# The last stage of a conditioned sequence block on one core: running sums by a scan, gate rows by transfers, one program for all blocks

## What is computed

```python
att = inputs @ attention_weights                       # [b, s, 16]
att = att - jnp.max(att, axis=1, keepdims=True)
att = jnp.exp(att * temperature)
v = jnp.einsum('bsi,ihk->bshk', inputs, values)
cumv = jnp.cumsum(v, axis=1)
denom = att * counts + EPS_ATT                          # counts = 1 .. s
attn_out = att[..., None] * cumv / denom[..., None]     # [b, s, 16, 64]
op = attn_out.reshape(b, s, 1024) @ operator + vector[:, None, :]
res = jax.nn.relu(jnp.concatenate([inputs, op], -1) @ ff1 + ff1_bias)
res = res @ ff2 + ff2_bias + inputs
# then a layer norm of res with gamma and beta
```

## Time and profile before

| | |
|---|---|
| median of 3 runs | 4029.58 us (4029.5 to 4034.14) |
| the profiled execution | 4030.17 us, span 4028.5 us |
| busy | TensorE 3595.8 us (89%), POOL 2282.0, DVE 2031.7, ACT 1588.7 |
| instructions | 50249 |

### The profile page before, as it was taken

The page is one execution under the profiler, slowest core; times in us unless marked ns, Lnnn a source line. Parts: engine busy times, 40 slices in busy tenths (PEclk is TensorE's granted clock), DMA queues, the critical chain, the costliest instruction groups (busy, mean ns, idle before and its releaser), DMA issues. The chain is left out here.

```text
span 4028.5 us, 50249 instructions
## 1 busy us (share of the span) xinstructions
PE 3595.8 (89%) x17632; PEld 2341.1 (58%) x17632; DVE 2031.7 (50%) x3302; ACT 1588.7 (39%) x2895; POOL 2282.0 (57%) x1776
## 2 busy tenths in 40 slices
PE   7996999999999999999999344999899957996998
PEld 6774445545544454444453333888688845875776
DVE  5652877767777677767773334111111133332333
ACT  3331366656666566666666113111111122221232
POOL 3555499979999799989999211222122232442443
PEclk9998799999999999999999677999899978997999
DMA  5546513103140304122100555011101121011010
GB/s 204 164 146 150 78 22 54 32 21 55 22 64 22 65 16 60 22 44 42 22 4 7 168 191 192 19 45 43 64 21 43 53 102 47 32 40 55 25 44 21
DMA packets 114748, 253.88 MB, mean 63 GB/s; under 512 B 12672, under 2 KB 13184, under 8 KB 108160
## 3 DMA queue, kind: packets, MB, share of 16 engines
q1 hardware_dynamic: 114496, 250.64, 23.9%
HBM read 155.17 MB, written 95.16 MB: 62 GB/s over the span
## 5 line engine op out<-in xcount | busy, mean ns | idle before, releaser
L714 DVE TENSOR_REDUCE part_max<-ps_att 128x1 f32<-128x512 f32 x2048 | 1271.7, 683 | 484.6 <-PE ps_att L633 484.3
L800 POOL TENSOR_TENSOR prob_sums<-prob_sums,probs 128x512 f32<-128x512 f32 x1152 | 1433.6, 1284 | 75.4 <-ACT probs L757 75.4
L757 ACT ACTIVATE probs<-ps_att 128x512 f32<-128x512 f32 x2048 | 1060.3, 603 | 585.0 <-PE ps_att L603 569.7
L603 PE MATMUL ps_att<-q_stack,k_stack 97*128 97x512 f32 x2048 | 867.4, 427 | 26.9 <-PEq L49 21.1
L633 PE MATMUL ps_att<-k_stack,q_stack 96*128 96x512 f32 x2048 | 831.6, 413 | 41.6 <-DMA k_stack<-qk 41.2
L603 PEld LDWEIGHTS ps_att<-q_stack,k_stack 97*128 97x128 f32 x2048 | 390.1, 191 | 503.6 <-ACT probs L757 286.7
L655 PE MATMUL ps_att<-probs,v_tok 128*32 128x512 f32 x4096 | 545.5, 605 | 0.0
L1247 POOL TENSOR_TENSOR ml_g_lo<-ml_g,ml_g_hi 128x512 fp32r<-128x512 f32 x128 | 164.8, 1287 | 649.0 <-DVE ml_g_hi L1223 649.0
L633 PEld LDWEIGHTS ps_att<-k_stack,q_stack 96*128 96x128 f32 x2048 | 400.2, 196 | 135.8 <-DMA k_stack<-qk 41.6
L1223 DVE CAST ml_g_hi<-ml_g 128x512 fp32r<-128x512 f32 x128 | 54.7, 427 | 571.8 <-ACT ml_g L1183 571.8
L1183 ACT ACTIVATE ml_g<-ps_mlp 128x512 f32<-128x512 f32 x128 | 76.5, 598 | 585.6 <-PE ps_mlp L1262 585.6
(11 more groups left out here) (192 smaller groups left out, 4765.6 us busy)
## 6 DMA issues: line engine op xcount, KB each, us to landing
q_stack<-qk SPq DMA_DIRECT2D x192, 128.0 KB, 4.4
k_stack<-qk SPq DMA_DIRECT2D x48, 512.0 KB, 19.4
qk<-rot_hi SPq DMA_DIRECT2D x64, 256.0 KB, 4.9
qk<-rot_lo SPq DMA_DIRECT2D x64, 256.0 KB, 3.2
x_in_sb<-in_x SPq DMA_DIRECT2D x8, 1024.0 KB, 8.4
v<-v_stage SPq DMA_DIRECT2D x8, 1024.0 KB, 4.4
v_tok<-v SPq DMA_DIRECT2D x8, 1024.0 KB, 32.0
yT<-o_sb SPq DMA_DIRECT2D x32, 256.0 KB, 2.5
```

The source lines that it names most:

```text
L603: nc.tensor.matmul(sT[u % 3], t["kS"][0:S3 + 1, b, h, k * P:(k + 1) * P], t["qS"][0:S3 + 1, h, n * TB:(n + 1) * TB], start=True, stop=True)\
L714: nc.vector.tensor_reduce(t["pm"][:, r, k:k + 1], mx[mx_uses % 3], AX.X, ALU.max)\
L757: nc.scalar.activation(t["p"][:, at % PR, h, :], sT[(at * G + h) % 3], ACT.Exp)\
L800: nc.gpsimd.tensor_tensor(x, first, t["p"][:, at % PR, h, :], ALU.add).then_inc(s["acc_done"], 1)
```

## The change

The three functions of the last stage become one, `average`, one block of program for all eight blocks of 512 tokens with no loop and no setup ahead of it.

- Running sums: DVE makes them from zT with one `tensor_tensor_scan` per 128 channels and block, each started with the carry; z is no longer cast, and the 32 staircase products, their tables and ACT's copies are gone.
- The gate is made on [128, 512] (16 heads x 4 blocks x 2 sequences), stored to DRAM, and each pair of heads gets its two rows spread over 128 partitions by a transfer, three buffers ahead. The product with the selector and ACT's copy are gone. The maximum that the exponential needs comes from the MLP stage, which takes it block by block and stores it at the end of each loop pass.
- Weights come in the order of their use (ff1, values, wp, ff2) into staging that is z's and zT's own buffers; the first three low parts are DVE's, the last three POOL's; TensorE starts with ff1's product as soon as that part is there.
- zT is loaded as 1 MB per block and kept whole. PSUM's eighth bank joins the ring of banks, now four.
- The four groups of `rows_out` follow one another, and all four row sums come before the four statistics; in the last block both halves are summed before the first is normalised.
- POOL makes the low parts of the running sums **before** those of the rectified rows.

```diff
@@ mlp @@
                         nc.vector.tensor_copy(at_sb[:], ps[0:H2, 6, :]).then_inc(s["att_out"], 1)
+                        dve.wait_ge(s["att_out"], n + 1)
+                        nc.vector.tensor_reduce(am[:, n:n + 1], at_sb[:], AX.X, ALU.max).then_inc(s["amax"], 1)
...
                     sp.wait_ge(s["att_stored"], 16 * NM)
+                    sp.wait_ge(s["amax"], NM)
+                    sp.dma_start(a["amax"][:, bass.ds(it * NM, NM)], am[:]).then_inc(s["amax_stored"], 16)
+                    sp.wait_ge(s["amax_stored"], 16)
@@ average: SP @@
+                def load_weight(i):
+                    if i >= 3:
+                        sp.wait_ge(s["w_lo"], i - 2)
+                    sp.dma_start(stage[i % 3], weights[i][0]).then_inc(s[f"w_in{i}"], 16)
...
+                def load_gate(v):
+                    n, h = v // HC, v % HC
+                    if v >= 3:
+                        sp.wait_ge(s["af"], v - 2)
+                    src = a["gate"][2 * h:2 * h + 2, n * TB:(n + 1) * TB].unsqueeze(1).broadcast_to([2, K2, TB])
+                    sp.dma_start(gb[:, v % 3, :], src).then_inc(s[f"g_in{v % 3}"], 16)
...
+                for n in range(NA):
+                    for h in range(HC):
+                        if n * HC + h + 3 < NA * HC:
+                            load_gate(n * HC + h + 3)
+                        if n and 1 <= h <= TT:
+                            store(n - 1, h - 1)
+                        if h == 0 and n + 1 < NA:
+                            load_zT(n + 1)
+                        if h == TT + 1 and n + 1 < NA:
+                            load_z(n + 1)
@@ average: TensorE @@
-            for n in range(NB + 1):
-                if n < NB:
-                    open_relu(n)
-                if n:
-                    rows_out(n - 1, 0)
-                    rows_out(n - 1, 1)
-                if n < NB:
-                    running_sums(n)
-                if n:
-                    rows_out(n - 1, 2)
-                    rows_out(n - 1, 3)
+                for n in range(NA + 1):
+                    if n < NA:
+                        open_relu(n)
+                    for j in range(TT if n else 0):
+                        rows_out(n - 1, j)
@@ average: DVE @@
+                def running_sums(n):
+                    dve.wait_ge(s[f"zT_in{n % 2}"], 16 * (n // 2 + 1))
+                    for f in range(DC):
+                        u = n * DC + f
+                        if u >= 2:
+                            dve.wait_ge(s["c_lo"], u - 1)
+                            dve.wait_ge(s["carry"], u - 1)
+                        begin = 0.0
+                        if n % NB:
+                            dve.wait_ge(s["carry"], u - DC + 1)
+                            begin = carry[:, (n - 1) % 2, f:f + 1]
+                        src, one = zTr[:, n % 2, f, :], c["ones"][:, 0:1].broadcast_to([P, TB])
+                        nc.vector.tensor_tensor_scan(cf[:, u % 2, :], one, src, begin, ALU.mult, ALU.add)\
+                            .then_inc(s["cf"], 1)
+                        if n and f == 0:
+                            dve.wait_ge(s["cumv"], HC * n)
+                        dve.wait_ge(s["cf"], u + 1)
+                        nc.vector.tensor_copy(ch[:, f, :], cf[:, u % 2, :]).then_inc(s["c_hi"], 1)
+                        nc.vector.tensor_copy(carry[:, n % 2, f:f + 1], cf[:, u % 2, TB - 1:TB])\
+                            .then_inc(s["carry"], 1)
@@ average: POOL @@
+                for n in range(NA + 1):
+                    for f in range(DC if n < NA else 0):
+                        u = n * DC + f
+                        pool.wait_ge(s["c_hi"], u + 1)
+                        nc.gpsimd.tensor_tensor(cl[:, f, :], cf[:, u % 2, :], ch[:, f, :].bitcast(F32), ALU.subtract)\
+                            .then_inc(s["c_lo"], 1)
+                    for i in range(LOW_POOL if n == 0 else len(weights), len(weights)):
+                        pool.wait_ge(s["w_hi"], i + 1)
+                        nc.gpsimd.tensor_tensor(weights[i][2], stage[i % 3], weights[i][1].bitcast(F32),
+                                                ALU.subtract).then_inc(s["w_lo_pool"], 1)
+                    for m in range(DC if n else 0):
                         u = (n - 1) * DC + m
                         pool.wait_ge(s["r_hi"], u + 1)
                         nc.gpsimd.tensor_tensor(sl[:, m, :], af[:, u % 2, :], sh[:, m, :].bitcast(F32),
                                                 ALU.subtract).then_inc(s["r_lo"], 1)
```

More of the change, by code:

```diff
@@ new lines, in average @@
+        s = {n[3:]: v for n, v in s.items()}
+        z_v = a["z"].rearrange("(n j p) f -> n p j f", n=NA, p=P)
+        out_v = a["out"].rearrange("(n j p) f -> n j p f", n=NA, p=P)
+        acc = [ps[:, i, :] for i in range(DC)]
+        ring = [ps[:, 4 + i, :] for i in range(4)]
+        bias = c["bias1"][:].rearrange("p (f b) -> p f b", b=B)
+        uses = []
+        for n in range(NA + 1):
+            uses += [("t", n - 1, j) for j in range(TT)] if n else []
+            uses += [("af", n, h) for h in range(HC)] if n < NA else []
@@ new lines, in average @@
+        at_use = {u: i for i, u in enumerate(uses)}
+        per_block = {"t": TT, "af": HC}
+        HALVES = (slice(0, 2), slice(2, TT))
+        parts = ((a["ff1"], fh, fl, slice(0, 4)), (a["values"], vh, vl, slice(0, 2)), (a["values"], vh, vl, slice(2, 4)),
+                 (a["wp"], wh, wl, slice(0, 4)), (a["wp"], wh, wl, slice(4, 8)), (a["ff2"], eh, el, slice(0, 4)))
+        weights = [[x[:, at, :].rearrange("p k n -> p (k n)") for x in (src, hi, lo)] for src, hi, lo, at in parts]
+        stage = [x.rearrange("p j f -> p (j f)") for x in (z[:, 0], z[:, 1], zTr[:, 1])]
@@ new lines, in variance, with rstd @@
+                def variance(n, js=slice(0, TT)):
+                    dve.wait_ge(s["stats"], TT * n + js.stop)
+                    for j in range(js.start, js.stop):
+                        nc.vector.bn_aggr(mv[:, j, :], st[:, j, :]).then_inc(s["aggr"], 1)
+                    dve.wait_ge(s["aggr"], TT * n + js.stop)
+                    nc.vector.tensor_scalar(va[:, js], mv[:, js, 1], EPS2, None, ALU.add).then_inc(s["var"], 1)
+                def rstd(part, js=slice(0, TT)):
+                    dve.wait_ge(s["root"], part + 1)
+                    nc.vector.reciprocal(rs[:, js], sd[:, js]).then_inc(s["rstd"], 1)
+                    dve.wait_ge(s["rstd"], part + 1)
@@ new lines, in _, with shifted @@
+            @block.gpsimd
+            def _(pool):
+                def shifted(n, j):
+                    pool.wait_ge(s["ga"], n * TT + j + 1)
+                    nc.gpsimd.tensor_tensor(z[:, n % 2, j, :], z[:, n % 2, j, :], be[:], ALU.add).then_inc(s["o"], 1)
+                for n in range(NA + 1):
+                    for f in range(DC if n < NA else 0):
[8 more added lines that the diff above has]
+                    for m in range(DC if n else 0):
@@ L1900, in laid_out @@
         "beta": np.ascontiguousarray(w["L1_cond_ln_beta"].reshape(1, D)),
[L1901 to L1902 removed]
+        "rotary": rotary_table(),
+        "counts": np.ascontiguousarray(np.tile(np.arange(1, L + 1, dtype=np.float32).reshape(NB, TB), (B * H2, 1))),
     }
```

714 lines of the change are left out of this document (288 added, 426 removed).

## The result

Measured together, the kernel before takes 4029.81 us (median of 4 runs, 4029.5 to 4034.14) and the changed one **3955.64 us** (4 runs, 3954.56 to 3957.72): ratio 0.9818, interval 0.9804 to 0.9832, 74 us less where 66 were forecast.

What follows compares the result with a forecast made beforehand. TensorE was taken as the bound inside a sequence. Block 0's heads end at 3389, seven periods (536 us) reach 3925, the tail 3958, the MLP adds 4.2: span 3962.4, so 3964 us, range 3914 to 3990.

Steps and rivals of the forecast that it cites:

- Step 1: TensorE products per block: 7.2 us removed, 66.5 us stay, plus 0.9 us between two blocks.
- Step 2: DVE scan of 1.2 us takes turns with POOL, 2.85 us each; opening products stall 6.2 us in each of seven blocks.
- Rival A: Scan does not exclude POOL: stall 1.8 us, period 70.5, total 3921 us; chance 0.25.
- rival B: Scan as slow as the reciprocal, 3.35 us: period 85.2, total 4024 us, no change that can be told; chance 0.04.
- Step 3: TensorE clock: a stall of 6 us per block brings one fall of the clock, +1.7 us.
- Step 4: Four row sums before four statistics on DVE: head 0's low part comes 1.3 us late instead of 0.5.
- Step 5: Gate-row loads on two DMA engines, 51 GB/s, 5.2 us each: nothing in steady state, some 5 us in block 0.
- Period: Time of one block: 66.5 + 0.9 + 6.2 + 1.7 + 1.3 = 76.6 us, nearly the 76.8 of before.
- Step 6: Start of the last stage: first transfer at about 3286.0, block 0's heads end at 3389.
- Step 7: End: seven more periods, 536 us, to 3925; tail of 30.5 us grows by 2.6, to 3958.
- Step 8: MLP: one more transfer in series at each end of two loop passes, 1.6 + 0.5 us each, +4.2 in all.
- Rival C: Slower by gate loads: one engine per load, 10.4 us each, 91 us per block, total 4106 us; chance 0.04.

Runs made afterwards that it cites:

- experiment 11: Changed kernel with POOL's old order, halved statistics, split gate transfers, new start, old tail order, last row products waiting for each rectified part alone; 3879.31 us.
- experiment 4: Changed kernel with each scan replaced by a plain DVE copy of the same rows, POOL's order kept; 3921.79 us.
- experiment 6: Changed kernel with row sums and statistics done for rows 0, 1 and then rows 2, 3 in every block; 3947.98 us.
- experiment 7: Changed kernel with each head's gate rows in two transfers of one DRAM row repeated 64 times, over 16 engines; 3952.16 us.
- experiment 8: Changed kernel with gate rows in transfers of 61 and 3 repeats, to put them on one engine; 4138.67 us, ratio 1.026.
- experiment 9: Changed kernel without the MLP's maxima and their transfer; the last stage takes its maximum over each partition's 512 logits itself; 3952.43 us.
- experiment 10: Changed kernel with rows 0 and 1 of the last block normalised before rows 2 and 3 are summed; 3954.07 us.

## Why the prediction was right, step by step

Sign, size and mechanism held; 3955.64 lies in the range.

- **Step 1, products**: with the waits gone (experiment 11) a period is 68.0 us for 66.5 + 0.9 forecast.
- **Step 2, scan and turns**: the scan was put at 1.2 us and takes 1.27; a turn was put at 2.85 and takes 2.63: beyond the scan, POOL's subtraction and the cast take 1.36 of it and not the 1.65 of the earlier trace rows. So the wait is 4.9 to 5.3 us, not 6.2. Rival A (the scan leaves POOL alone) is refuted by the 2.31 us scan and by experiment 4, rival B by the 1.27 us. (The 1.8 us of rival A come out as 1.4 when the count is done with turns of 1.65; 3 us of its total.) On the two pages of the Trainium skill that were cited: the trace agrees with the Trainium skill's "SBUF — State Buffer" (section SBUF: two separate sides) for the scan too, 2.31 us under a POOL instruction, and with the half throughput in the Trainium skill's "DVE: opcode table, instruction layouts, handler registers and perf-mode slots" (section Datapath and trigger behaviour), 1.27 us for what would be an estimate of 1.2.
- **Step 3, clock**: one fall of the clock per block, as forecast; it costs 2.2 us on average and not 1.7, and between 1.6 and 3.0 from block to block.
- **Step 4, statistics**: head 0's low part was to come 1.3 us late; TensorE waits 0.97 us for it, and with the statistics in halves the wait is gone and the period is about 1.1 shorter (experiment 6).
- **Step 5, gate rows**: two engines and 51 GB/s, read in the window (columns as before):

```profile
3464.00:3470.00 6.00, 4.38 (x20) 3.29 (x18) 5.93 (x7) 0.55 (x1) 5.10 (x3) 1.00 0.13 51
```

  They cost nothing from block 1 on and about 5 us in block 0 (experiment 7), as forecast. The runs agree with the rule of the Trainium skill's "DMA: Bandwidth & Descriptors" (Why a DMA increments its semaphore by 16 and not by 1): a DMA share of 0.13 for 2 rows here, of 0.79 while two of experiment 7's transfers with 64 repeats ran (3495.5 to 3497.0), of 0.07 for 61 repeats in experiment 8 (3609 to 3616).
- **Period**: 76.4 for 76.6. The terms were off by -1.1 (wait), +0.5 (clock), -0.3 (statistics) and +0.6 (products and the 0.9 between blocks, 68.0 for 67.4), and nearly cancel; that the period is met within 0.2 us is luck in part, the wait in its place and of its size is not.
- **Step 6, start**: the term that was off most. Block 0's heads were to end at 3389 + 4.2 for the MLP and end at 3385.1, 8 us earlier: 1.2 of it lie ahead of the first transfer (it left at 3289.03, for 3286.0 + 4.2) and are the MLP's (experiment 9), 7 are the start's own. The rows of the changed kernel show where:

```profile
3318.24 2.28 DVE L1599 TENSOR_TENSOR val_lo<-av_z_sb,val_hi 128x2048 fp32r<-128x2048 f32 x1
3320.44 3.35 DVE L1599 TENSOR_TENSOR val_lo<-av_zT,val_hi 128x2048 fp32r<-128x2048 f32 x1
...
3332.69 4.52 POOL L1721 TENSOR_TENSOR ff_lo<-av_zT,ff_hi 128x2048 fp32r<-128x2048 f32 x1
3337.16 1.26 POOL L1731 TENSOR_TENSOR av_gated_lo<-av_full,av_gated_hi 128x512 fp32r<-128x512 f32 x1
```

  Counted from the first transfer, DVE was through with the running sums after 29.2 us (32 in the forecast), with the two weight parts after 34.8 (43), head 0's low part was there after 49.4 (56.7), and the heads ended after 96.1 (103). Most of it is the price of the two weight parts, 11 us where they took 5.6: a POOL subtraction of 5.5 us was put between them, and POOL's first was in fact issued behind DVE's last. The path was another too: head 0's low part did not wait for the sixth part's load but for POOL, which was busy with the fourth and fifth part for 11.1 us from 3321.6 on and then with the sixth for 4.52, not 5.5.
- **Step 7, tail**: 34.5 us for 33.1. Of the 4.1 us above before, the reordering is 2.8 (experiment 10; from the start of the last four row products to POOL's last addition 11.5 us pass after the change and 8.7 before), 0.7 are row products that run longer at the low clock behind the last rectifications, and 0.6 pass after POOL's last addition.
- **Step 8, MLP**: 1.5 and 1.4 us at the two passes' ends for 2.1 each.
- **Rival C**: real as a mechanism (experiment 8), and even dearer than its price, but the loads ran on two engines.

Two things stay open: periods of the changed kernel vary between 75.7 and 77.4 us, nearly all of it in the stretch at low clock behind the wait, and why that stretch is longer in some blocks was not tested; and experiment 11 met its sum (3880), but its new start and the row products' own waits were not run one by one.

## What to carry to other kernels

When products leave the engine that bounds a kernel, look at the places where it waits at all: the order of a third engine's queue can give the whole saving back, and here five lines of order were worth 54 us. Where two engines lock each other out, price an operation by the turns that stand ahead of the first instruction someone waits for, not by its own length: in one order each microsecond of the scan cost nearly four of waiting, and the wait a fall of the clock; in the other, scans done twice cost nothing after the first block. A transfer that is hidden is hidden per buffer, so compare one load with one head, not all of them with a block.

## What was not expected

- Behind a cast DVE's scan starts first (3462.25) and POOL's subtraction 0.1 us later (3462.35), and the later one carries both durations: 2.27 us instead of 1.29. A long POOL operation in a trace may be a DVE operation that it stands behind.
- A weight subtraction of 128x2048 takes POOL 4.5 to 4.6 us when DVE has no more than a gate multiplication beside it (4.52 for the sixth part; 4.63 for the fifth in experiment 11), and 6.62 when it starts under DVE's last one (the fourth part there). The 5.5 us each of the earlier trace rows, from which step 6 priced it, are the mean of two such cases: the first of the pair took 6.53 us, under DVE's subtraction, and the second 4.51.
- In experiment 8 one engine moved the gate rows at 25 to 26 GB/s (3609 to 3616), and the issues of the gate loads on SP took 1.9 us each in the median (0.6 in experiment 11), some 10 us each group of four. The output stores, which stand behind such a group in SP's queue, left late as well.
